# Three quarters of a feed-forward weight matrix split in the last steps of the self-attention before it, and the order of the feed-forward's first operations

## What is computed

```python
# self-attention, 16 heads of 32, causal with a decay mask
qkv = ln(x) @ w_attn                       # w_attn 512 x 1536
att = softmax(q @ k.T / sqrt(32) + mask)
x = x + (att @ v) @ w_proj                 # w_proj 512 x 512
# feed-forward
h = float2fix(ln(x) @ w1 + b1)             # w1 512 x 2048
h = float2fix(piecewise_linear_gelu(h))
x = x + float2fix(h @ w2 + b2)             # w2 2048 x 512
```

## Time and profile before

| | |
|---|---|
| time, median of 3 runs | 1675.73 us (1671.87 to 1675.92) |
| profiled execution, its own time | 1676.23 us |
| its span, first to last instruction | 1674.3 us |
| busy, share of the span | PE 96%, DVE 74%, ACT 61%, POOL 48% |
| self-attention's code ends, feed-forward begins | 1260.5 us after the span's start |
| first group of the feed-forward, up to the end of up(16) | about 1260.5 to 1372.8 us |

### The profile page before, as it was taken

How to read it: one execution, slowest core, us unless ns; L and a number is a source line. 1 busy time by engine, 2 the same in 40 slices (tenths; PEclk the granted TensorE clock), 3 DMA queues, 4 the chain that set the end, 5 groups by cost and what they waited for, 6 DMA issues and landing times. The chain is left out here.

```text
span 1674.3 us, 30263 instructions
## 1 busy us (share of the span) xinstructions
PE 1613.0 (96%) x11142; PEld 1396.7 (83%) x11142; DVE 1232.5 (74%) x2381; ACT 1029.0 (61%) x2036; POOL 798.3 (48%) x747
## 2 busy tenths in 40 slices
PE   6999999999999999999999999999977999999998
PEld 4888899998989999898998779889865777878786
DVE  5548878788787878888785945566656987777776
ACT  3348777777777777777784414454445665656554
POOL 3216545464555546455452322334334666455555
PEclk9999999999999999999999999999987999999999
DMA  8783434434343443535345840112113221010010
GB/s 266 225 236 98 134 94 114 118 105 134 98 135 95 113 119 105 135 99 135 106 111 172 287 145 14 46 58 77 58 45 89 82 63 57 19 57 13 20 38 26
DMA packets 173687, 173.38 MB, mean 104 GB/s; under 512 B 80930, under 2 KB 138338, under 8 KB 173540
## 3 DMA queue, kind: packets, MB, share of 16 engines
q1 hardware_dynamic: 173540, 171.45, 35.1%
HBM read 133.65 MB, written 37.75 MB: 102 GB/s over the span
## 5 line engine op out<-in xcount | busy, mean ns | idle before, releaser
L75 PE MATMUL p_bank_score<-p_ctxt,p_qo 128*128 128x256 f32 x2304 | 304.5, 286 | 1.0 <-ACT p_probs L999 0.7
L75 PEld LDWEIGHTS p_bank_score<-p_ctxt,p_qo 128*128 128x128 f32 x2304 | 288.0, 191 | 6.2 <-issue 2.4
L75 PE MATMUL p_bank_mix<-p_probt,p_ctx 128*128 128x512 f32 x1152 | 292.1, 398 | 0.5
L75 PEld LDWEIGHTS p_bank_mix<-p_probt,p_ctx 128*128 128x128 f32 x1152 | 207.4, 189 | 41.9 <-issue 3.8
L1962 PE MATMUL p_bank_down<-p_w,p_ht 128*128 128x512 f32 x768 | 198.1, 405 | 1.8 <-DVE p_ht L2049 1.8
L1920 POOL TENSOR_TENSOR p_a<-p_a,p_g 128x512 f32<-128x512 f32 x64 | 111.8, 1746 | 160.4 <-ACT p_a L2000 160.4
L1196 DVE SCALAR_TENSOR_TENSOR p_qo<-p_bank_mix,p_odd,p_qo 128x512 fp32r<-128x512 f32 x192 | 143.8, 749 | 57.4 <-ACT p_qo L1013 49.8
L705 POOL TENSOR_TENSOR p_ctx<-p_ctx_in,p_ctx 128x768 fp32r<-128x768 f32 x64 | 118.5, 1851 | 131.7 <-ACT p_ctx L988 131.4
L1962 PEld LDWEIGHTS p_bank_down<-p_w,p_ht 128*128 128x128 f32 x768 | 143.6, 190 | 40.1 <-issue 4.8
L1013 ACT ACTIVATE p_qo<-p_bank_mix,p_odd 128x512 fp32r<-128x512 f32 x192 | 132.6, 690 | 67.9 <-PE p_bank_mix L75 67.3
L999 ACT ACTIVATE p_probs<-p_bank_score,p_small 128x257 f32<-128x257 f32 x256 | 121.7, 476 | 58.6 <-DVE p_small L1177 54.4
(11 more groups left out here) (276 smaller groups left out, 3692.3 us busy)
## 6 DMA issues: line engine op xcount, KB each, us to landing
p_blocks_in<-in_ctx_dram SPq DMA_DIRECT2D x256, 96.0 KB, 2.4
p_ctx_in<-in_ctx_dram SPq DMA_DIRECT2D x64, 384.0 KB, 3.1
q<-p_ctx SPq DMA_DIRECT2D x64, 256.0 KB, 3.2
p_odd_in<-in_ctx_dram SPq DMA_DIRECT2D x64, 192.0 KB, 3.4
p_x<-in_x_dram SPq DMA_DIRECT2D x32, 256.0 KB, 4.3
p_quad<-q SPq DMA_DIRECT2D x32, 256.0 KB, 3.9
p_probt<-q SPq DMA_DIRECT2D x32, 256.0 KB, 4.4
p_o_in<-o SPq DMA_DIRECT2D x8, 1024.0 KB, 7.3
```

Of the source, the lines that this page charges most:

```text
L75: made = e.matmul(out, lhsT, rhs, start=n == 0, stop=n == last)
```

## The change

Three edits. (1) The 12 blocks of w1 that were split in the feed-forward are split in the self-attention's steps 14, 15 and 16, four in each, over four raw buffers that lie where q tiles are no longer used. The halves go where `w_attn` lay, which now outlives the self-attention. A block's load waits for the low half of the block four before it. (2) The feed-forward splits only w2: blocks 0 and 1 in step 0, then one a step to step 14. (3) In the feed-forward's first step the rounding of `m` stands first on VectorE; the rest of the layer norm's statistics, the split of b2 and block 0 come behind it, and SP loads b1 and b2 ahead of the blocks.

The hunks on late blocks are, in order: SP's loads; GpSimd, ahead of the low half of `yt`; ScalarE, ahead of `y_raw` and ahead of the high half of `yt`; VectorE, ahead of the transpose and ahead of the residual.

```diff
+        LATE = {NT - 2: (0, 4), NT - 1: (4, 4), NT: (8, 4)}
+        late_raw = [raws[:, i, :] for i in range(4)]
...
+                for k in late_blocks(t + 2, (0, 1)):                  
+                    if k == 0:
+                        e.wait_ge(scored, NB * (NT - 2))
+                    if k >= 4:
+                        e.wait_ge(late_odd if k % 2 else late_even, k // 2 - 1)
+                    e.dma_start(late_raw[k % 4], late_block(k)[1]).then_inc(late_in[k % 4], DMA)
                 e.wait_ge(added, t + 1)
...
+                for k in late_blocks(t, (1,)):
+                    low_late(k)
...
+                for k in late_blocks(t, (0, 1))[0:2]:
+                    high_late(k)
...
+                for k in late_blocks(t, (0, 1))[2:]:
+                    high_late(k)
...
+                for k in late_blocks(t, (0,))[0:1]:
+                    low_late(k)
...
+                for k in late_blocks(t, (0,))[1:]:
+                    low_late(k)
...
-        EARLY = 2
-        blocks = []
-        for c in range(F // C):
-            if c > 0:
-                blocks += [(w_1[k * P:(k + 1) * P, c * C:(c + 1) * C], w1[:, :, k, (c - 1) * C:c * C])
-                           for k in range(KT)]
-            blocks += [(w_2[k * P:(k + 1) * P, :], w2[:, :, k, :])
-                       for k in range(c * C // P, (c + 1) * C // P)]
+        blocks = [(w_2[k * P:(k + 1) * P, :], w2[:, :, k, :]) for k in range(KF)]
...
-            return [k for k in range(EARLY + 2 * n, min(EARLY + 2 * n + 2, len(blocks))) if lane in (None, k % 2)]
+            return [k for k in range(n + (n > 0), min(n + 2, KF)) if lane in (None, k % 2)]
...
-            norm.prepare(e, 1)
-            low_block(0)
-            e.wait_ge(b2_hi, 2)
+            norm.guard(e, 1)
```

More of the change, by code:

```diff
@@ L1361, in self_attention @@
         w_raw = room.sb("w_raw", [P, C])
+        with ExitStack() as second:
+            raws = second.enter_context(nc.sbuf_tensor("p4_late_raw", [P, 4, C], F32))
         qts = room.ring("q", 2, [P, 2, NM, G], F32R)
@@ L1388, in self_attention, with late_block, late_blocks @@
         projected, added, y_seen = room.sems("projected", "added", "y_seen")
+        late_in = room.sem_ring("late_in", 4)
+        late_hi, late_even, late_odd = room.sems("late_hi", "late_even", "late_odd")
         SEEN, WEIGHTS = 6, range(7, 7 + KT)
+        LATE = {NT - 2: (0, 4), NT - 1: (4, 4), NT: (8, 4)}
+        late_raw = [raws[:, i, :] for i in range(4)]
+        def late_block(k):
+            c = k // KT + 1
+            return wattn[:, :, k % KT, (c - 1) * C:c * C], w_1[k % KT * P:(k % KT + 1) * P, c * C:(c + 1) * C]
+        def late_blocks(t, lanes):
+            first, count = LATE.get(t, (0, 0))
+            return [k for k in range(first, first + count) if k % 2 in lanes]
         uses = [("q", 0), ("q", 1), ("k", 0), ("k", 1), ("v", 0), ("v", 1)]
@@ L1464, in scale_rows, with low_late @@
                 after.norm.scale(e, i - NT, xs[i % 3][:])
+            def low_late(k):
+                hi, lo = (late_block(k)[0][:, h] for h in (HI, LO))
+                e.wait_ge(late_hi, k + 1)
+                e.tensor_tensor(lo, late_raw[k % 4], f32(hi), ALU.subtract).then_inc(late_odd, 1)
             for j, part in enumerate(parts):
@@ L1601, in high_values, with high_late @@
                 e.activation(vs[n % 4][:, HI, :], bank_of("v", n), ACT.Copy).then_inc(v_hi, 1)
+            def high_late(k):
+                e.wait_ge(late_in[k % 4], DMA * (k // 4 + 1))
+                if k == 0:
+                    e.wait_ge(valued, NT)
+                e.activation(late_block(k)[0][:, HI], late_raw[k % 4], ACT.Copy).then_inc(late_hi, 1)
             norm.root(e, 1)
@@ L1666, in low_values, with low_late @@
                                 ALU.subtract).then_inc(v_lo, 1)
+            def low_late(k):
+                hi, lo = (late_block(k)[0][:, h] for h in (HI, LO))
+                e.wait_ge(late_hi, k + 1)
+                e.tensor_tensor(lo, late_raw[k % 4], f32(hi), ALU.subtract).then_inc(late_even, 1)
             norm.guard(e, 1)
@@ L1752, in self_attention, with feed_forward @@
             block.sync(sync)
-def feed_forward(nc, ahead, x2_dram, w_1, b_1, w_2, b_2, out_rows):
+def feed_forward(nc, ahead, w1, x2_dram, w_1, b_1, w_2, b_2, out_rows):
     G = 512
@@ L1771, in feed_forward @@
         norm = ahead.norm
-        w1 = room.sb("w1", [P, 2, KT, F - C], F32R)
         w2 = room.sb("w2", [P, 2, KF, C], F32R)
@@ L1949, in down @@
                 if g == 0:
[L1950 removed]
+                    blocks_are_split(e, f + 1)
                 if n == 0:
@@ L1980, in scalar @@
             e.activation(scratch[:], quarter[:], ACT.Gelu).then_inc(ready, 1)
[L1981 to L1985, removed]
             for n in range(NT + 1):
@@ L2000, in scalar @@
                     e.activation(a[:], v[:], ACT.Gelu, bias=quarter[:]).then_inc(gelu1, 1)
+                    if n == 0:
+                        e.wait_ge(b2_in, 2 * DMA)
+                        e.activation(b2_pair[0:1, :], b2[0:1, :], ACT.Copy).then_inc(b2_hi, 1)
+                        e.activation(b2_pair[QUAD:PAIR, :], b2[QUAD:PAIR, :], ACT.Copy).then_inc(b2_hi, 1)
                     for k in blocks_at(n, None):
@@ L2106, in build @@
                            x2_moments, ended)
-        feed_forward(nc, after, x2_dram, L0_ffn_w1, L0_ffn_b1, L0_ffn_w2, L0_ffn_b2, out_rows)
+        feed_forward(nc, after, wattn, x2_dram, L0_ffn_w1, L0_ffn_b1, L0_ffn_w2, L0_ffn_b2, out_rows)
 _INS = ["x", "ctx_768", "L0_xattn_w_q", "L0_xattn_w_k", "L0_xattn_w_v", "L0_xattn_w_o",
```

18 lines of the change are left out of this document (8 added, 10 removed).

## The result

| kernel | time, us, median of runs | ratio to before, 95% interval | profiled execution | its span |
|---|---|---|---|---|
| before | 1675.83 (1671.87 to 1676.49, 6 runs) | | 1676.23 | 1674.3 |
| changed | 1680.59 (1678.84 to 1681.34, 6 runs) | 1.0031 [1.0019, 1.0044] | 1680.49 | 1678.7 |

The changed kernel is slower by 0.3%, where I had forecast 1673.0. Start of up(0) on PE, S, is now at 1268.51; step 14's scores begin at 1221.56 in this trace and at 1221.66 in that of before, so everything up to there took the same time and the two can be laid side by side.

What follows compares the result with a forecast made beforehand. It took VectorE to bound the feed-forward's first group, PE all later ones, and one chain the self-attention's end. Feed-forward -9.7 and tail +6.9 gave -2.8 us on 1676.23: 1673.4, as a median 1673; 8 in 10 range 1667.5 to 1680.

Steps and rivals of the forecast that it cites:

- Start of the feed-forward: Feed-forward's first step: first rounding 2.2 us earlier, at S+4.3, but PE's idleness and low clock nearly stay; gain 0.7 us.
- The other steps of the first group: Feed-forward, down(0) to the end of up(16): 83.0 instead of 92.0 us, 9.0 less, if VectorE keeps up.
- rival C: First group: VectorE lags over 4 us in places, PE pauses once or twice, gain falls by 4.4: 1677.5; chance 0.13.
- the rule on GpSimd and VectorE that I cited for the tail: Steps 14 to 16: moved low halves on VectorE and POOL add up without overlap; the tail's 9 us end, not 3.5.
- Steps 14 and 15: Self-attention's steps 14 and 15: moved halves delay the end of tile 15's `pt` low from 1246.3 to 1247.6, +1.3 us.
- Step 16: Self-attention's last step: late loads and moved halves delay `yt` low from 1251.38 to 1258.3, +6.9 us for all that follows.
- Rival A: Self-attention's end: blocks 8 and 9 are in before ACT gets there, tail costs only 3.5: 1669.5; chance 0.19.
- Rival B: First group: in-order waits between DVE, ACT and POOL keep each step at 6.27, gain of 9.0 lost: 1682; chance 0.12.
- D: Clock: pauses in the tail make PE slow; slow matmuls for all of up(0) cost 1: 1674; 0.56 together with the forecast.
- The sum: Whole kernel: -9.7 + 6.9 = -2.8 us on the profiled 1676.23, giving 1673.4; median 0.5 lower, 1672.9.

Runs made afterwards that it cites:

- e5: The changed kernel again, unchanged, as a control on the chip of the next three runs; 1680.99 us, 1.0026 of the kernel before.
- e1: Changed kernel with the third edit undone: statistics, block 0 and b2 again ahead of the first rounding; 1678.14 us, 1.0012 of the kernel before.
- e3: Changed kernel with w2's blocks split two in each even step, none in odd ones, same work in all; 1677.63 us, 0.9997 of the kernel before.
- e2: Changed kernel with POOL writing zeros instead of subtracting for w2's odd blocks' low halves in the feed-forward; 1676.71 us, 1.0006 of the kernel before.
- e7: Changed kernel with eight raw buffers, moved blocks mostly behind the tile's own operations, and w2's blocks in pairs; 1666.95 us, 0.9944 of the kernel before.
- e4: Changed kernel with eight raw buffers instead of four for the moved blocks, blocks 4 to 11 loaded one step earlier; 1675.49 us, 0.9992 of the kernel before.
- e6: Changed kernel, four buffers kept, last step's four blocks behind the last yt on ACT and POOL, ahead of VectorE's last residual; 1675.64 us, 0.9999 of before.

## Why the prediction was wrong

*Start of the feed-forward*, 0.7 us gained: the timing was right, the gain was not there. The first rounding came at S+4.40 (forecast 4.3) and the second 7.57 later (7.4); but down(0) came 0.3 us earlier in one execution and 0.9 later in the other (e5), and earlier with the third edit undone (19.38, e1) than with it in either. PE's idle time, 7.53 us, and the low clock behind it stayed, as said.

*The other steps of the first group* is the step that failed: "That is 9.0 us less, if VectorE keeps up. It does by its own sum." The group gave 4.3. I took 4.5 us for a step without a block from a trace in which each step had held POOL's work within it, and 6.27 for one with a block, and added them up to 71. That sum is right for the operations: e3, with the same ones in pairs, takes 71.1, and e2 70.7. But blocks alternated one a step. The 4.55 us step was too short for POOL, whose work spilled into the next, the very one with a block, and held up VectorE's operations there. The five such steps took 7.67, 8.08, 7.03, 9.08 and 8.08 us. Four of them also carry work for a row tile, which the forecast counted apart; the one without, step 9, shows the spill alone, 7.03 instead of 6.27, and it is largest in step 11. The steps came to 75.7, 4.7 more than 71, and as much as the group missed of its 83.0 (87.65). It is rival C in size (4.4) and C's mechanism, a lag of VectorE, but PE did not stall twice for 2.8 us with a slow clock; it lost 0.4 to 1.1 at a time at full clock, since the lag grows by little in each pair of steps. What I had not priced is the next group, 1.1 us more up to up(20), where PE waits for VectorE twice instead of once. In part it may be an echo of the spill: without the spill the first of the two waits is 0.26 or 0.27 us instead of 1.03 (e2, e3, e7), and the stage 23.34 in e2 and e7. But it was 24.34 in e3, with PE at the low clock behind the second wait (0.67 granted), so this part is not shown.

The Trainium skill, "SBUF — State Buffer", "Who interferes with whom", has the rule on GpSimd and VectorE that I cited for the tail. The trace agrees with it where I did not apply it: an operation of VectorE with two inputs that began beside POOL's lasted until 0.54 or 0.55 us behind its end, in three cases of three in step 11. The same section names the one-input kind of `p_v` too as one that can be kept out, and the odd steps bear it out.

*Steps 14 and 15*, +1.3 at `pt` low: it ended at 1248.08 instead of 1247.6, +1.8. Block 5's load was late too, which I had not seen: ACT waited for it until 1243.12.

*Step 16*, +6.9: the mechanism was right and its size 1.1 us short. `y_raw` came at 1254.41 (forecast 1253.3), `yt` low at 1259.30 (1258.3), S at 1268.51 (1267.4). The term that was mis-sized is the landing: I took 2.6 us from single loads and pairs, and in a burst of four, issued at 1249.67, the first was in at 1252.8 and the second at 1253.9; the median was 4.0. One reason that I gave was not the binding one: block 9 hardly waited for POOL's block 5 (1248.03 + 1.5) but stood behind SP's store of tile 13, which came at 1249.30, 2.4 us later than in the earlier trace rows, and behind block 8. Rival A fell because of the loads, but its price was good: with the loads early (e4) the moved operations cost 3.8 us at the last projection, against its 3.5, and 2.3 at S, since that projection ran at the full clock.

*Rival B* fell: steps without a block did last 4.55. *D*: the last projection was as slow as before the change (4.58), so it cost nothing new; e4 and e6 show that 1.6 us are to be had there. D's price of 1 us for a slow up(0) is what e5 shows, 1.2.

*The sum.* Of the 7.1 us by which the profiled execution missed 1673.4, 4.7 are the spill, 1.1 the next group, 1.1 the tail, and 0.4 the start, less 0.2 of what lies outside the stages.

## What to carry to other kernels

A helper engine's work for a step takes its time even if the step becomes shorter: before pricing a step at what is left when work is taken out, see whether the other engines' operations still end within it, and on which operations of the next step they fall. Work that is moved into an idle stretch belongs behind the operations of the chain that ends there, not ahead; behind them late loads cost nothing, and only ahead of them do the loads have to be early. From the same twelve blocks e4, with early loads, got 5.8 us back, and e6, which moved four of them behind and left the loads late, 7.8. Moving work and placing it are two changes; here the move was worth 0.56% and its first placing cost 0.8% of the time.

## What the hardware showed that I had not expected

- A VectorE operation on SBUF data that starts beside a GpSimd tensor-tensor operation ends at a constant distance behind it, as if it had run almost wholly after it: 0.54 to 0.55 us for those of 0.69 with two inputs, 0.15 or 0.16 for the one of 0.29 on `p_v` (1309.63 + 1.75 and 1310.45 + 1.09; 1347.03 + 1.43 and 1347.95 + 0.66). The rounding, whose data lie in PSUM, is not held up: 0.74 us at 1345.64, beside GpSimd's operation of 1345.12 to 1346.88, as ever.
- GpSimd's write of 128x512 zeros took 0.53 us, and the `p_v` operation beside it ended 0.14 us behind it (e2, step 11). A two-input operation beside such a write was not held up: 0.69 us at 1295.52, beside the write of 1295.28 to 1295.95 (e2).
- A 256 KB load landed in 2.6 us where few were issued at once, in 4.0 (median of nine) where they came in bursts of four, and in 5.8 (e4) and 5.4 (e7), medians of twelve, where eight of the twelve came in one burst.
- After a pause of 1.16 us (e4) PE took 3.03 us for 12 matmuls, after 1.80 (e7) 4.59, after 2.88 (changed) 4.58; but after 2.51 it took 5.84 for 24 (e6). The granted clock was 1.00 in the first and the last, 0.63 in the other two. The length of the pause alone doesn't tell whether slow matmuls follow.
